# Layer 0 of a two-layer attention kernel: maxima taken by width, narrow units as one event, mask products with a 64-column identity

## The chip, the cores and the metric

One Trainium2 chip, one of its cores. The metric is device microseconds (us) of one execution of the whole program; lower is better. A core has five engines that run their own instruction lists and wait for each other by semaphores: PE (TensorE, matmuls into the PSUM banks), DVE (VectorE), ACT (ScalarE), POOL (GpSimd) and SP (SyncE, which here only issues DMAs).

## The reference, cut to what matters

```python
# B = 2 sequences of T = 1024 tokens, model width 128
x = x + retention(x)                 # 8 heads, not touched by the change
# layer 0: 16 heads of 8 dimensions, causal
scores = jnp.einsum('bhqd,bhkd->bhqk', q, k) / np.sqrt(HEAD_DIM)
scores = jnp.where(causal, scores, -jnp.inf)
attn = jax.nn.softmax(scores, axis=-1)
out = jnp.einsum('bhqk,bhkd->bhqd', attn, v) ...
# then 4 experts (argmax routing)
# layer 1: 16 heads of 8, not causal; two corner scores are set to -1e9
scores = scores.at[:, :, 0, -1].set(NEG)
scores = scores.at[:, :, -1, 0].set(NEG)
weights = jax.nn.softmax(scores, axis=-1)
# then a 128x128 ternary product
```

The layer-0 causal mask matters here: a tile of 128 queries needs only the keys up to its own, so the score blocks have widths of 128, 256, 384 or 512 columns.

## The kernel before, in words

The attention of both layers works in **stacks**: a layer, a batch and a group of four heads. A stack has two **blocks** m, one for each half of 512 queries (`c = m % 2`), so layer 0 has blocks 0 to 15. A block is cut in **units** by tiles of 128 keys: 4 units where c is 0, 8 where c is 1 (layer 1 always has 8). The units of all blocks stand in one list `us`; layer 0 has 96 of them (8 stacks of 12), layer 1 has 128. The loop of `order()` runs over **steps**, one per unit, and writes the program order that PE, ACT and DVE all follow.

In a step s there are, for each of two head pairs x:

- `("S", (s, x))`: PE makes the scores of the unit, keys by queries, two matmuls that stand in the two halves of the array's rows (`par` 0 and 1, one head each; L1525). On the diagonal four more matmuls add the causal mask (L1533): each multiplies 64 rows of two stored tables and adds up to 128 columns. ACT then makes exp of them (L1711), one instruction per head. Three PSUM banks hold scores, so a pair waits for the first exp of the pair before it.
- `("A", (u, x))`: PE makes scores again, queries by keys, for a unit u that lies 12 units ahead (L1453, mask L1460), and DVE reduces them to the maxima (L1886, one instruction for two heads). These go through a **ring** of two slots of two banks each, shared with all other small PE products: a matmul waits until the use two places before it has been read.
- `("V", (s - 1, x))`: PE multiplies the exps of the unit before by V, for one half of the 512 queries (L1559, four heads).

Twelve units are one stack, so unit u of step s is the same unit of the next stack. What `("A", u)` computes is chosen by `maxima_of`: before, blocks with c = 0 take their query tiles upwards (widths 128, 256, 384, 512) and blocks with c = 1 take the two key halves in turn (512, 128, 512, 256, 512, 384, 512, 512). The score units have the widths 512, 384, 256, 128 and five times 512, then 384, 256, 128.

When the maxima of a block are complete, `("M", m)` turns them on PE (L1502), ACT copies them (L1779), POOL splits them in three parts and sends them by three DMAs into the query rows of the stack (L1321). The first score unit of the block waits for these. `("O", m)` (L1567) turns the block's output; the copy of the finished output bank by ACT (L1724) must be done before the first V of the next block. SP loads the query and key rows of later stacks when score counts are reached.

Of the kernel before, what the change touches and what calls it, by code (L numbers as in the profile page):

```python
# [17 lines left out]
P = 128  # L18
# [41 lines left out]
def constants():  # L60
# [131 lines left out]
def build(nc, d, out, phases=5):  # L192
    ctx = ExitStack()
    with ctx:
# [866 lines left out]
        def order():  # L1061
# [75 lines left out]
        def attention():  # L1137
# [263 lines left out]
            def _(pe):  # L1401
# [9 lines left out]
                for kind, k in order():  # L1411
# [21 lines left out]
                    elif kind == "A":  # L1433
# [17 lines left out]
                        for par in range(2):  # L1451
                            rows = slice(HALF * par, HALF * par + SROWS)
                            ins = nc.tensor.matmul(bank(first + par)[:, 0:hi - lo], Qs[k_][rows, qc, x, qo:qo + P],  # L1453
                                                   Ks[k_][rows, x, lo:hi], start=True, stop=not (diag or corner))
                        o = qt * P - lo if diag else (384 if qt == 0 else 0)
                        terms = ((0, 2), (1, 3)) if diag else (((4, 5),) if qt == 0 else ((6, 7),)) if corner else ()
                        for z, (one, two) in enumerate(terms):
                            for par in range(2):
                                rows = slice(HALF * par, HALF * (par + 1))
                                ins = nc.tensor.matmul(bank(first + par)[:, o:o + P], masks[rows, one, :],  # L1460
                                                       masks[rows, two, :], start=False, stop=z == len(terms) - 1)
# [41 lines left out]
                    elif kind == "S":  # L1503
# [9 lines left out]
                        q = HG * s + 2 * x  # L1513
                        ready(pe, exp_done, q + 2 - SCORES)
                        if x == 0 and kt == 0:
                            if m == 1:
                                warm(bank(S_BANK + q % SCORES), 8)
# [5 lines left out]
                        for par in range(2):  # L1523
                            rows = slice(HALF * par, HALF * par + bottom)
# [580 lines left out]
```

## Time and profile before

| | |
|---|---|
| median of 3 runs | 1038.59 us (1037.97 to 1040.91) |
| the profiled execution: time, span | 1032.61 us, 1030.6 us |
| PE busy, share of the span | 905.3 us, 88% |
| DVE | 764.5 us, 74% |
| ACT | 661.7 us, 64% |
| POOL | 391.0 us, 38% |
| mean granted PE clock | 0.965 of 2.4 GHz |
| layer 0's score units | from 294.15 to 627.02 us |

The profile is of one execution; its times are microseconds from the span's start. A busy share says how long an engine had work, not whether the work set the pace. Matmuls overlap, so what counts for PE is the time from one group's start to the next one's start.

### The profile page before, as it was taken

Reading aid. Unit: us, or ns where it says so; the run is one execution under the profiler, and the core shown is the slowest. Engines: PE = TensorE matmul, PEld = TensorE weight load, DVE = VectorE, ACT = ScalarE, POOL = GpSimd, SP = SyncE. Lnnn points to the kernel's source line nnn. Section 1 sums busy time; section 2 is a strip of 40 time slices with the busy share of each in tenths; the row PEclk is TensorE's granted clock in tenths of the full one; section 3 lists DMA queues with packets and bytes.
Section 4 is the critical chain, followed back from the end, with each engine's and each line's share of the span. In section 5 each row is a group of like instructions: output and inputs, shape, how many; then the busy total and the mean of one; then the engine's idle time right before and its main releaser. Section 6 shows DMA issues by size and latency. Waiting matters only on the chain.

```text
span 1030.6 us, 22869 instructions
## 1 busy us (share of the span) xinstructions
PE 905.3 (88%) x9065; PEld 451.3 (44%) x9070; DVE 764.5 (74%) x1187; ACT 661.7 (64%) x1349; POOL 391.0 (38%) x607
## 2 busy tenths in 40 slices
PE   5999999998878888988798878889989999999983
PEld 3778777777523343344373322325422222222232
DVE  3667766856586678867457688796789999999854
ACT  2554565655435677766545647776668988898971
POOL 2755757877332451223444302342423111211240
PEclk8999999999988999999898999999999999999996
DMA  8000000200501034111320431022205100000000
GB/s 291 1 1 2 1 1 2 73 1 2 148 1 41 21 127 136 38 39 37 111 81 23 144 74 37 5 76 91 84 1 169 49 20 20 20 20 2 4 23 21
DMA packets 49405, 52.51 MB, mean 51 GB/s; under 512 B 8874, under 2 KB 40618, under 8 KB 49140
## 3 DMA queue, kind: packets, MB, share of 16 engines
q1 hardware_dynamic: 45012, 48.12, 15.2%
q0 software_dynamic: 4288, 2.94, 1.1%
q8 instruction: 72, 1.18, 0.5%
q14 instruction: 33, 0.27, 0.1%
HBM read 32.37 MB, written 19.68 MB: 51 GB/s over the span
## 4 chain that ended last, share of the span: by engine, by line
PE 50%; DVE 28%; ACT 8%; issue 6%; POOL 3%; DMA 3%; SPq 1%; DVEq 0%; ACTq 0%; POOLq 0%
DVE arena L1886 21%; PE banks L1559 10%; PE banks L1525 7%; PE banks L1453 4%; ACT arena L1711 4%; PE banks L740 3%; PE banks L485 3%; PE banks L495 2%; PE banks L1634 2%; PE banks L1642 2%; PE banks L673 2%; PE banks L735 1%; PE banks L699 1%; ACT arena L521 1%; PE banks L723 1%
## 5 line engine op out<-in xcount | busy, mean ns | idle before, releaser
L1711 ACT ACTIVATE arena<-banks 128x512 f32<-128x512 f32 (+3 forms) x896 | 444.5, 550 | 144.1 <-PE banks L1525 83.9
L1886 DVE TENSOR_REDUCE arena<-banks 128x2 f32<-128x1024 f32 (+1 forms) x448 | 474.8, 1105 | 83.5 <-PE banks L1460 51.5
L1559 PE MATMUL banks<-arena 128*9 128x256 f32 (+1 forms) x3328 | 257.7, 383 | 8.1 <-ACT arena L1724 5.7
L1525 PE MATMUL banks<-arena 61*128 61x512 bf16 (+4 forms) x896 | 170.0, 371 | 29.7 <-ACT arena L1711 26.3
L1453 PE MATMUL banks<-arena 56*128 56x512 bf16 (+3 forms) x896 | 166.7, 366 | 26.8 <-DVE arena L1886 23.3
L1525 PEld LDWEIGHTS banks<-arena 61*128 61x128 bf16 (+1 forms) x896 | 44.8, 93 | 195.0 <-ACT arena L1711 174.5
L1311 POOL CAST arena<-arena 16x128 bf16<-16x128 f32 x32 | 8.9, 279 | 309.3 <-ACT arena L1779 305.3
L1559 PEld LDWEIGHTS banks<-arena 128*9 128x9 f32 x3328 | 50.4, 89 | 134.7 <-issue 83.1
L1453 PEld LDWEIGHTS banks<-arena 56*128 56x128 bf16 x896 | 45.2, 96 | 53.9 <-DVE arena L1886 47.0
L383 POOL TENSOR_TENSOR arena<-arena 128x8 f32<-128x8 f32 (+1 forms) x35 | 51.3, 1466 | 30.8 <-DVE arena L2050 28.4
L1321 POOL DMA_DIRECT2D arena<-arena x96 | 55.1, 577 | 10.7 <-POOL arena L1314 9.2
L521 ACT ACTIVATE arena<-banks,arena 128x128 f32<-128x128 f32 x128 | 46.3, 476 | 0.5 <-PE banks L504 0.5
L1460 PE MATMUL banks<-arena 64*128 64x128 bf16 x576 | 45.4, 226 | 0.0
L511 ACT ACTIVATE arena<-banks 128x1024 f32<-128x1024 f32 x16 | 16.3, 1022 | 39.9 <-PE banks L740 39.9
L1351 POOL DMA_INDIRECT expert_rows<-arena x22 | 21.3, 970 | 54.4 <-DVE arena L1982 54.4
L554 DVE TENSOR_TENSOR arena<-banks,arena 128x128 f32<-128x128 f32 x16 | 4.6, 290 | 47.0 <-PE banks L495 47.0
L1533 PE MATMUL banks<-arena 64*128 64x128 bf16 x512 | 38.8, 219 | 0.0
L529 ACT ACTIVATE arena<-banks 128x1024 f32<-128x1024 f32 x16 | 16.4, 1025 | 33.9 <-PE banks L485 32.6
L767 DVE TENSOR_TENSOR arena<-banks,arena 128x1024 f32<-128x1024 f32 x16 | 19.5, 1221 | 24.2 <-PE banks L673 24.1
L485 PE MATMUL banks<-arena 128*128 128x128 f32 x256 | 34.2, 289 | 2.6 <-DVE arena L770 2.6
L673 PE MATMUL banks<-arena 128*128 128x512 f32 x64 | 33.0, 641 | 1.9 <-DMA arena<-c_gk 1.9
L1460 PEld LDWEIGHTS banks<-arena 64*128 64x128 bf16 x576 | 29.3, 100 | 12.3 <-issue 2.2
(235 smaller groups left out, 1392.6 us busy)
## 6 DMA issues: line engine op xcount, KB each, us to landing
arena<-k_products SPq DMA_DIRECT2D x32, 224.0 KB
arena<-q_products SPq DMA_DIRECT2D x64, 112.0 KB
q_products<-arena SPq DMA_DIRECT2D x16, 384.0 KB, 3.3
k_products<-arena SPq DMA_DIRECT2D x16, 384.0 KB, 3.8
arena<-e_w SPq DMA_DIRECT2D x22, 256.0 KB, 3.1
arena<-arena POOLq DMA_DIRECT2D x96, 4.0 KB, 1.7
sorted_rows<-c_pads SPq DMA_DIRECT2D x2, 709.5 KB, 8.2
arena<-sorted_rows SPq DMA_DIRECT2D x4, 258.0 KB, 3.2
```

The source lines that it names most:

```text
L383: link(eng.tensor_tensor(y, v, epst[:, 1:2].to_broadcast(list(v.shape)), ALU.pow))
L485: ins = nc.tensor.matmul(bank(s // 4)[:, (s % 4) * P:(s % 4 + 1) * P], wg[:, s * P:(s + 1) * P], XT[:, i, :], start=True, stop=True)
L521: ins = nc.scalar.activation(ga[:, s, :], bank(4 + s // 4)[:, (s % 4) * P:(s % 4 + 1) * P], ACT.Identity, scale=gn[:, 0, s:s + 1], bias=gn ...
L673: ins = nc.tensor.matmul(bank(c), XT[:, n + 1, :], wqk[:, c * 512:(c + 1) * 512], start=True, stop=True)
L1321: g_.dma_start(rows, nmp[k % 2][:, i, :]).then_inc(mrow[k % 2], 16)
L1453: ins = nc.tensor.matmul(bank(first + par)[:, 0:hi - lo], Qs[k_][rows, qc, x, qo:qo + P], Ks[k_][rows, x, lo:hi], start=True, stop=not (di ...
L1460: ins = nc.tensor.matmul(bank(first + par)[:, o:o + P], masks[rows, one, :], masks[rows, two, :], start=False, stop=z == len(terms) - 1)
L1525: ins = nc.tensor.matmul(bank(S_BANK + (q + par) % SCORES)[:, o:C], Ks[n % NS][rows, x, kt * P:(kt + 1) * P], Qs[n % NS][rows, c, x, o:C], ...
L1533: ins = nc.tensor.matmul(bank(S_BANK + (q + par) % SCORES)[:, o:o + P], masks[rows, 2 + z, :], masks[rows, z, :], start=False, stop=z == 1)
L1559: ins = nc.tensor.matmul(PS[h * VROWS:h * VROWS + VW, AV_BANK, o:end], V[:, b, kt, HG * g + h, :], Pr[u % PROBS][:, h, o:end], start=(kt = ...
L1711: s_.activation(Pr[s % PROBS][:, h, o:C], bank(S_BANK + q % SCORES)[:, o:C], ACT.Exp) \
L1886: v_.tensor_reduce(of, two_banks, AX.X, ALU.max).then_inc(ring_dve, 1)
```

## The change

Four edits, all in the attention part.

1. `maxima_of` gives layer 0's maxima in the widths 512, 384, 256, 128 (c = 0) and four times 512, then 512, 384, 256, 128 (c = 1). In layer 0 a unit's maxima now have the width of the score unit in the same step, nearly throughout.
2. Units at most 256 wide (`narrow_scan`) put both head pairs into one ring use, one behind the other in each bank: one reduction with four results per partition in place of two. Layer 0 has 32 such units.
3. Score units at most 256 wide (`narrow`) do the same: one pair of banks holds four heads, and ACT makes two exps of 2x256 or 2x128 in place of four. `score_use` numbers the pairs of banks, `exps_of` the counts to wait for.
4. The causal mask is now a table times a 64-column identity: the same number of matmuls, each 64 columns wide in place of 128. The corner masks of layer 1 keep their tables and widths.

```diff
@@ constants()
-        step = HALF * k + lane[:, None] + 1
-        m[:, k] = r[None, :] < step
-        m[:, 2 + k] = np.where(r[None, :] >= step, MASKED, 0)
+        step = HALF * k + lane[:, None]
+        m[:, k] = np.where(step > r[None, :], MASKED, 0)
+        m[:, 2 + k] = np.where(r[None, :] > step, MASKED, 0)
@@ maxima_of
-            return (j, 0) if tiles(m) == QT else (QT * c + j // 2, j % 2)
+            if m < BLOCKS:
+                return (QT * (c + 1) - 1 - j % QT, c if j // QT == c else 0)
+            return QT * c + j // 2, j % 2
@@ new, beside it
+        def narrow(m, kt):
+            lo, hi = queries(m, kt)
+            return hi - lo <= C // 2
+        def narrow_scan(m, j):
+            qt, kc = maxima_of(m, j)
+            return m < BLOCKS and kc == m % 2 and qt % QT < QT // 2
+        score_use, exps_of = {}, []
+        for s, (m, kt) in enumerate(us):
+            for x in range(HG // 2):
+                if x == 0 or not narrow(m, kt):
+                    score_use[s, x] = len(exps_of)
+                    each = 2 if narrow(m, kt) else 1
+                    exps_of += [HG * s + 2 * x + each, HG * s + 2 * x + 2 * each]
@@ order()
-                pairs = [("A", (u, x)) for u in scans.get(s, []) for x in range(2)]
+                pairs = [("A", (u, x)) for u in scans.get(s, []) for x in range(1 if narrow_scan(*us[u]) else 2)]
-                    if 0 <= s < NU:
+                    if (s, x) in score_use:
                         seq.append(("S", (s, x)))
-                    seq += pairs[x * len(pairs) // 2:(x + 1) * len(pairs) // 2]
+                    seq += pairs[(x * len(pairs) + 1) // 2:((x + 1) * len(pairs) + 1) // 2]
@@ PE, "A" and (alike) "S"
+                        for y in range(2) if narrow_scan(m, j) else (x,):
+                            at = y * C // 2 if narrow_scan(m, j) else 0
...
+                            for z in range(2 * diag):
+                                for par in range(2):
+                                    rows, cut = slice(HALF * par, HALF * (par + 1)), at + o + HALF * z
+                                    ins = nc.tensor.matmul(bank(first + par)[:, cut:cut + HALF], masks[rows, z, :],
+                                                           identb[rows, rows], start=False, stop=z == 1)
@@ ACT, "S"
+                            if narrow(m, kt):
+                                s_.activation(Pr[s % PROBS][:, par:HG:2, o:C],
+                                              scores.rearrange("p (y e) -> p y e", y=2)[:, :, 0:C - o], ACT.Exp) \
+                                  .then_inc(exp_done, HG // 2)
@@ DVE, "A"
+                        if both:
+                            v_.tensor_reduce(of, two_banks.rearrange("p r (y e) -> p r y e", y=2)[:, :, :, 0:width],
+                                             AX.X, ALU.max).then_inc(ring_dve, 1)
```

PE's list at the end of block 5, of before: units 6 and 7 (scores 256 and 128 wide, L1525) and the first half of unit 0 of block 6. The maxima (L1453) of these steps are 512 wide, then 128.

```order
L1525 MATMUL banks<-arena 128x256 x2
L1533 MATMUL banks<-arena 128x128 x4
L1453 MATMUL banks<-arena 128x512 x2
L1559 MATMUL banks<-arena 9x256 x4
L1525 MATMUL banks<-arena 128x128 x2
L1533 MATMUL banks<-arena 128x128 x4
L1453 MATMUL banks<-arena 128x512 x2
L1460 MATMUL banks<-arena 128x128 x4
L1525 MATMUL banks<-arena 128x128 x2
L1533 MATMUL banks<-arena 128x128 x4
L1453 MATMUL banks<-arena 128x512 x2
L1460 MATMUL banks<-arena 128x128 x4
```

The same place of the changed kernel, from unit 7 on (L1557 and L1566 are the scores and their mask, L1477 and L1487 the maxima and theirs, L1592 the V products).

```order
L1557 MATMUL banks<-arena 128x128 x2
L1566 MATMUL banks<-arena 128x64 x4
L1557 MATMUL banks<-arena 128x128 x2
L1566 MATMUL banks<-arena 128x64 x4
L1477 MATMUL banks<-arena 128x128 x2
L1487 MATMUL banks<-arena 128x64 x4
L1477 MATMUL banks<-arena 128x128 x2
L1487 MATMUL banks<-arena 128x64 x4
L1592 MATMUL banks<-arena 9x256 x4
L1557 MATMUL banks<-arena 128x512 x2
```

Both head pairs of a narrow unit now stand together, the maxima of the step have shrunk from 512 to 128 columns, and the V products follow without scores between them.

DVE's list around the first steps of the attention, of before: the reductions (L1886), the work for the last retention tile among them (L542 to L1878), and the joining of a block's maxima (L1893).

```order
L1886 TENSOR_REDUCE arena<-banks 128x2 x4
L542 TENSOR_TENSOR arena<-arena 128x1024
L1886 TENSOR_REDUCE arena<-banks 128x2 x2
L554 TENSOR_TENSOR arena<-banks,arena 128x128
L556 BN_STATS arena<-arena 128x6
L557 BN_AGGR arena<-arena 128x2
L1878 MEMSET banks 128x512
L1886 TENSOR_REDUCE arena<-banks 128x2 x2
L1893 TENSOR_TENSOR arena<-arena 128x16
L1886 TENSOR_REDUCE arena<-banks 128x2 x16
```

And of the changed kernel (L1930 is a reduction of one head pair, L1927 one of both).

```order
L1930 TENSOR_REDUCE arena<-banks 128x2 x4
L542 TENSOR_TENSOR arena<-arena 128x1024
L1927 TENSOR_REDUCE arena<-banks 128x4
L554 TENSOR_TENSOR arena<-banks,arena 128x128
L556 BN_STATS arena<-arena 128x6
L557 BN_AGGR arena<-arena 128x2
L1917 MEMSET banks 128x512
L1927 TENSOR_REDUCE arena<-banks 128x4
L1937 TENSOR_TENSOR arena<-arena 128x16
L1930 TENSOR_REDUCE arena<-banks 128x2 x12
```

The four reductions ahead of L542 were 128, 128, 256 and 256 wide and are now 512, 512, 384 and 384; the narrow ones come behind it.

## Rows read from the trace of the kernel before

**Rows 1.** The page: the chain that ended last, by engine.
```profile
PE 50%; DVE 28%; ACT 8%; issue 6%; POOL 3%; DMA 3%; SPq 1%; DVEq 0%; ACTq 0%; POOLq 0%
```

**Rows 2.** By stretch: us, busy PE, PEld, DVE, ACT, POOL; PE clock, DMA.
```profile
396.00:406.00 10.00, 10.00 (x147) 3.95 (x145) 8.59 (x11) 8.13 (x18) 0.02 (x1) 1.00 0.66 208
296.00:306.00 10.00, 8.51 (x91) 3.47 (x93) 8.65 (x11) 5.13 (x12) 1.51 (x5) 0.66 0.01 2
```

**Rows 3.** Timeline, units 2 and 3 of block 5: start, us, engine, line.
```profile
394.59 0.39 PE L1525 MATMUL banks<-arena 59*128 59x512 bf16 x2
396.81 0.39 PE L1525 MATMUL banks<-arena 59*128 59x512 bf16 x2
```

**Rows 4.** Timeline of PE, units 6 and 7 of block 5.
```profile
404.51 0.28 PE L1525 MATMUL banks<-arena 59*128 59x256 bf16 x2
404.63 0.28 PE L1533 MATMUL banks<-arena 64*128 64x128 bf16 x4
404.74 0.38 PE L1453 MATMUL banks<-arena 56*128 56x512 bf16 x2
405.05 0.41 PE L1559 MATMUL banks<-arena 128*9 128x128 f32 x8
405.44 0.28 PE L1525 MATMUL banks<-arena 59*128 59x256 bf16 x2
...
406.54 0.23 PE L1525 MATMUL banks<-arena 59*128 59x128 bf16 x2
...
407.39 0.23 PE L1525 MATMUL banks<-arena 59*128 59x128 bf16 x2 [0.18 <-ACT arena L1711]
...
408.02 0.62 PE L1559 MATMUL banks<-arena 128*9 128x256 f32 x8
```

**Rows 5.** Timeline of PE, unit 0 of block 6 and what follows.
```profile
408.57 0.39 PE L1525 MATMUL banks<-arena 59*128 59x512 bf16 x2
...
409.91 0.39 PE L1525 MATMUL banks<-arena 59*128 59x512 bf16 x2 [0.66 <-ACT arena L1711]
...
411.08 0.34 PE L1525 MATMUL banks<-arena 59*128 59x384 bf16 x2
```

**Rows 6.** Timeline, block 4: M for block 5, its DMAs, units 2, 3, next block.
```profile
381.35 0.28 PE L1502 MATMUL banks<-arena 128*16 128x128 f32 x1
...
384.36 0.28 PE L1525 MATMUL banks<-arena 59*128 59x256 bf16 x2
...
384.56 1.70 POOL L1321 DMA_DIRECT2D arena<-arena  x3 [0.29 <-POOL arena L1314]
...
386.46 0.23 PE L1525 MATMUL banks<-arena 59*128 59x128 bf16 x2
...
389.06 0.39 PE L1525 MATMUL banks<-arena 59*128 59x512 bf16 x2
```

**Rows 7.** Timeline of PE, units 0 and 1 of block 5.
```profile
391.56 0.28 PE L1502 MATMUL banks<-arena 128*16 128x128 f32 x1 [0.33 <-DVE arena L1886]
...
392.69 0.23 PE L1453 MATMUL banks<-arena 56*128 56x128 bf16 x2 [0.53 <-DVE arena L1886]
```

**Rows 8.** Groups by form, 290 to 600 us: count | busy, mean ns.
```profile
L1886 DVE TENSOR_REDUCE arena<-banks 128x2 f32<-128x1024 f32 x95 | 112.3, 1220 | 21.8 <-PE banks L1453 17.2 <-PE banks L1460 3.7
L1886 DVE TENSOR_REDUCE arena<-banks 128x2 f32<-128x256 f32 x29 | 12.3, 424 | 13.2 <-PE banks L1460 13.1
```

**Rows 9.** Timeline: eight matmuls at most 32 columns wide, each with own weights.
```profile
485.85 0.34 PE L1610 MATMUL banks<-arena 128*128 128x32 bf16 x8
```

**Rows 10.** Timeline of PE: waits for DMAs in blocks 11 and 15.
```profile
502.43 0.63 PE L1619 MATMUL banks<-arena 128*128 128x128 f32 x4 [1.53 <-DMA arena<-sorted_rows]
...
596.84 0.61 PE L1453 MATMUL banks<-arena 56*128 56x512 bf16 x4 [0.15 <-DMA arena<-q_products]
```

**Rows 11.** Timeline of PE: M for block 1, and block 1's first unit.
```profile
305.70 0.28 PE L1502 MATMUL banks<-arena 128*16 128x128 f32 x1
...
313.65 0.39 PE L1525 MATMUL banks<-arena 59*128 59x512 bf16 x2 [0.98 <-DMA arena<-arena]
```

More of the change, by code:

```diff
@@ L1450, in _ @@
                         qc, qo = qt // QT, qt % QT * P
[L1451 to L1454, printed above, removed]
                         o = qt * P - lo if diag else (384 if qt == 0 else 0)
-                        terms = ((0, 2), (1, 3)) if diag else (((4, 5),) if qt == 0 else ((6, 7),)) if corner else ()
@@ L1522, in _ @@
                         bottom = MROWS if m < BLOCKS else EROWS
-                        for par in range(2):
-                            rows = slice(HALF * par, HALF * par + bottom)
-                            ins = nc.tensor.matmul(bank(S_BANK + (q + par) % SCORES)[:, o:C],
-                                                   Ks[n % NS][rows, x, kt * P:(kt + 1) * P],
-                                                   Qs[n % NS][rows, c, x, o:C], start=True, stop=not diag)
-                            if not diag:
-                                ins.then_inc(score_done, 1)
@@ L1530, in _ @@
-                        for z in range(2 * diag):
-                            for par in range(2):
-                                rows = slice(HALF * par, HALF * (par + 1))
-                                ins = nc.tensor.matmul(bank(S_BANK + (q + par) % SCORES)[:, o:o + P], masks[rows, 2 + z, :],
-                                                       masks[rows, z, :], start=False, stop=z == 1)
-                                if z == 1:
-                                    ins.then_inc(score_done, 1)
+                        both = narrow(m, kt)
@@ new lines, in _ @@
+                        for y in range(2) if both else (x,):
+                            at = y * C // 2 if both else o
+                            done = HG // 2 if both else 1
+                            for par in range(2):
+                                rows = slice(HALF * par, HALF * par + bottom)
+                                ins = nc.tensor.matmul(bank(S_BANK + (use + par) % SCORES)[:, at:at + C - o],
+                                                       Ks[n % NS][rows, y, kt * P:(kt + 1) * P],
+                                                       Qs[n % NS][rows, c, y, o:C], start=True, stop=not diag)
+                                if not diag:
+                                    ins.then_inc(score_done, 1)
+                            for z in range(2 * diag):
+                                for par in range(2):
+                                    rows = slice(HALF * par, HALF * (par + 1))
+                                    cut = at + HALF * z
+                                    ins = nc.tensor.matmul(bank(S_BANK + (use + par) % SCORES)[:, cut:cut + HALF],
+                                                           masks[rows, 2 + z, :], identb[rows, rows], start=False, stop=z == 1)
+                                    if z == 1 and (y == 1 or not both):
+                                        ins.then_inc(score_done, done)
```

42 lines of the change are left out of this document (26 added, 16 removed).

## The prediction

> **What bounds the kernel now.** I read the page first. The chain that ended last lies half on PE, 28% on DVE and 8% on ACT [rows 1]: no engine sets the pace everywhere, so a busy share can't price this change. I then split layer 0 into stretches. From 396 to 406 us PE is busy throughout, DVE for 8.59 and ACT for 8.13 of 10 us, at the full clock, 2.4 GHz [rows 2]. The reader should see three engines almost equally loaded: an engine that gets a wide piece while another has a narrow one makes the other wait. The timeline shows it step by step. A wide step without masks takes 2.22 us (394.59 to 396.81) [rows 3]; its two reductions take 2.44 us of DVE [rows 8], so DVE only keeps up by catching up elsewhere. The narrow score units 6 and 7 of block 5 take 2.03 us each (404.51 to 406.54 to 408.57) [rows 4, 5], nearly as much as a wide one, though their scores are a half and a quarter as wide. They carry maxima of 512 columns, and in unit 7 PE waits for ACT [rows 4]. In block 4, units 2 and 3 take 2.10 and 2.60 us (384.36, 386.46, 389.06) [rows 6]. Right behind them PE waits for DVE, 0.33 us for M and 0.53 us for a slot of the ring [rows 7]: DVE is still working through wide reductions that it got in the narrow steps.
>
> **PE's prices**, from group start to group start [rows 4]: a 256-wide pair 0.12 us (404.51 to 404.63), a mask group of four 0.11 (to 404.74), a 512-wide pair and the step to V 0.31 (to 405.05). V over 128 queries takes 0.39 (to 405.44), over 256 queries 0.55 (408.02 to 408.57) [rows 4, 5]. By columns a 128-wide pair costs 0.06; each 128 columns are 0.05; the step to V then costs 0.09.
>
> **The mask groups.** They keep four matmuls and four weight loads, and halve the columns. No row shows 64-column groups. If columns set the price, 0.11 becomes 0.055; if the number of instructions does, it stays 0.11. The nearest row has eight matmuls with own weights, at most 32 columns wide, in 0.34 us including the last one's way through the array, some 0.17 by a comparison with the 0.23 of a 128-wide pair [rows 4, 9]; so about 0.02 each, 0.08 for four. I take 0.08, a saving of 0.03 for each group, with 0 and 0.055 as ends.
>
> The trace has the mask group at 0.11 us. The Trainium skill, page "TensorE: Matmul & The Clock Gate", section Back-to-back issue gap, puts a floor of about 25 ns under the distance of two matmuls however few columns they have. By it four masks would cost 0.10 us, and the halved columns would give almost nothing; no run shown so far has the 64-column form.
>
> **The steps of a stack, one by one.**
> - Unit 6 of an odd block: scores 2x0.12, maxima 2x0.12 (they were 512 wide), four mask groups at 0.08, 0.09, V 0.39+0.55: 1.83 against 2.03, saves 0.20.
> - Unit 7: 2x0.06, 2x0.06, 4x0.08, 0.09, 0.55: 1.20 against 2.03, saves 0.83. The next scores wait for the first exp of this unit; from scores through exp to scores took 1.34 us at 512 columns (408.57 to 409.91 [rows 5]), and this exp has 256 elements, so the chain should end before 1.20.
> - Units 2 and 3 of an even block are the same two: 1.83 against 2.10 and 1.20 plus 0.57 (O, by 2.60 less 2.03) against 2.60: save 0.27 and 0.83.
> - Unit 0 of an even block: 2.51 us (408.57 to 411.08), its first half bound by scores, exp, scores (the 0.66 us wait for ACT [rows 5]). Maxima grow from 128 to 512 columns: +0.16 in the half that is not covered, masks -0.09: +0.07. Unit 1: 256 becomes 384 and masks shrink: 0.
> - Units 0 and 1 of an odd block: DVE has now had a 256- and a 128-wide unit before, so both waits for it (0.86 us together [rows 7]) can go; but V of unit 1 then waits for ACT's copy of the finished output, which starts behind the same exps. I take 0.45, between 0 and 0.86.
> - Units 2 and 3: the masked 256-wide maxima become unmasked 512 ones, +0.10 and -0.11: 0. Units 4 and 5: masks, 0.06 and 0.12.
>
> An even block saves 1.03 us, an odd one 1.66, a stack 2.7. Merging by itself removes the fixed part of 32 reductions and 64 exps (two 256-element reductions take 0.85 us [rows 8]); it lies beside PE's work in these steps and is costed at nothing. Were PE no cover, it would be worth some 0.2 us in each narrow unit.
>
> **What lies in the way.** The narrow steps hid the chain of M. M for block 5 stands at 381.35, its DMAs at 384.56, the block's scores at 389.06: 7.71 us [rows 6]. Mine leaves 7.71-0.27-0.83 = 6.6. The chain itself takes 3.21 us to the DMAs and 1.70 to issue them, 4.9, and then the landing, for which at most 2.8 us were left; so it needs between 4.9 and 7.7 us. I take the middle, 6.3: just covered. At the upper end an odd block would lose 1.1 us.
>
> **The sum over layer 0.** Stacks 1 to 4 save 2.7 each: 10.8. In stack 5, PE waits 1.53 us for the sorted rows [rows 10]; POOL's scatter sets that, so what units 2 and 3 of block 10 and unit 0 of block 11 save before it (1.4) only lengthens the wait: 1.3 is left. In stack 6, what comes after block 13's unit 6 is lost: layer 1's first maxima wait for a store and a load (0.15 us at 596.84 [rows 10]), and faster steps meet that wait: 1.9 is left. Stack 7 gives nothing: it runs under that chain, and then under layer 1's double scans, which DVE bounds. In stack 0, block 1 saves 1.7. Block 0 saves nothing: its steps end in a wait for M's DMAs, 7.95 us behind M (305.70 to 313.65) [rows 11]. DVE gets 2048 elements more before the last retention tile's work (widths 128 and 256 become 512 and 384), at (1220-424)/768 = 1.04 ns each [rows 8] 2.1 us, and as many fewer behind it. I take 0 for that, with 2 us either way.
>
> Total: 10.8+1.3+1.9+1.7 = 15.7 us. Against the profiled execution's 1032.6 us that is 1016.9; the median of the runs is 6.0 us above it, so 1022.9, say 1023.
>
> **Rivals.**
> - *Half of it* (20%): 3 to 10 us, 1028 to 1035. Masks that stay at 0.11 take 0.03 from some 28 groups in each of six stacks, 5 us; DVE, which then bounds units 0 to 5 of odd blocks (2.44 us a unit against 2.22), keeps the 0.45, 3 us more; M's chain could come on top. For it: three engines this evenly loaded leave a gain on one little room. Against it: unit 7's 0.83 rests on columns that are simply gone from there.
> - *Nothing* (5%): the program keeps its columns but for the masks, so if PE's columns were the whole price, moving them would give only 0.03 a group, and the ring's order could eat that. Against it: unit 7 and unit 3 hold waits and maxima that don't come back elsewhere in full, since a step bound by ACT or DVE takes the wider maxima in its slack [rows 5, 7].
> - *Slower* (4%): PE's clock. Between 296 and 306 us the mean grant is 0.66, a mixture of 1.2 and 2.4 GHz, after PE had waited for ACT and DVE; ten such microseconds hold 3.4 us of lost clock [rows 2]. If narrower matmuls made the clock fall in blocks that now run at 2.4 GHz, one such stretch in a block would cost up to 3.4 us. From five of them in fourteen blocks on, the change loses. Against it: the steps get shorter by losing waits, and 396 to 406 us runs at 1.00 with these waits near it.
>
> The Trainium skill's page "TensorE: Matmul & The Clock Gate", section Part 1, says that the throttled clock is the default and activity releases it. By that rule fuller narrow steps should keep the clock; the 0.66 stretch agrees as far as it goes.
> - *More* (8%): over 23 us saved, 1015 or less. The mask groups go to 0.055 (4 us more), both DVE waits go whole (3 us), and the start gains 2.
>
> **How the numbers follow.** The forecast's own case, 10 to 23 us saved, has 63%. The unknown mask price alone moves the sum by 5 us down or 4 up, the start by 2, the DVE waits by 3. The range leaves out under 1 in 10 on each side: 1013 to 1032. A change of 0.3% (3.1 us) is about what a measurement of this kernel can tell. Faster by more than that: 63+8 and 20 of the half case, 91%; same 5%; slower 4%.
>
> **What the changed profile would show.** Reductions: 416 in place of 448, 16 of them 1024 and 16 of them 512 elements in four results. Unit 6 of a steady odd block near 1.8 us and unit 7 near 1.2; unit 3 of an even one near 1.8; the waits for DVE in units 0 and 1 gone or moved to ACT's copy. Mask groups 0.08 us from start to start. The wait for sorted rows longer, near 3 us. Layer 1 unchanged in length from its first maxima on. I am wrong if units 1 to 3 of odd blocks grow past 2.4 us (DVE is then the bound), if block starts wait for M's DMAs by 0.5 us or more, or if the clock column falls below 1.00 in blocks 3 to 9.

## The result and the profile after

| | before | after |
|---|---|---|
| median (lowest to highest) | 1038.28 us (1036.71 to 1040.91, 4 runs) | 1023.83 us (1023.12 to 1026.3, 4 runs) |
| ratio | | 0.9857, 95% interval 0.9829 to 0.9885 |
| profiled execution, its span | 1032.61, 1030.6 us | 1024.54, 1022.1 us |
| mean granted PE clock of it | 0.965 | 0.957 |

The change saves 14.5 us between the medians. The profiled executions differ by only 8.1 us: the one of before is 5.7 us below its median, and the one of after holds a stall of 4.7 us in layer 1 that other executions of the same kernel don't have (below). Measured again beside the kernel before, the change saved 16.0 us and, another time, 10.8 us, so the size of the gain is itself uncertain by some microseconds. The page of after, its chain by engine and its groups:

```profile
PE 50%; DVE 27%; ACT 7%; issue 6%; DMA 4%; POOL 3%; SPq 2%; another core or an unknown queue 1%; DVEq 0%; ACTq 0%; POOLq 0%
...
L1930 DVE TENSOR_REDUCE arena<-banks 128x2 f32<-128x1024 f32 (+1 forms) x384 | 440.9, 1198 | 65.4 <-PE banks L1477 33.0
...
L1927 DVE TENSOR_REDUCE arena<-banks 128x4 f32<-128x1024 f32 (+1 forms) x32 | 30.4, 954 | 16.2 <-PE banks L1487 13.5
L1746 ACT ACTIVATE arena<-banks 128x512 f32<-128x512 f32 (+1 forms) x64 | 27.9, 490 | 17.2 <-PE banks L1566 16.9
```

384 and 32 are the 416 reductions that were expected; the chain keeps its shares [rows 1]. Units 6 and 7 of block 5 and the start of block 6, timeline of PE (answers to [rows 4, 5]):

```profile
398.23 0.28 PE L1557 MATMUL banks<-arena 59*128 59x256 bf16 x2
398.35 0.22 PE L1566 MATMUL banks<-arena 64*128 64x64 bf16 x4
398.41 0.27 PE L1557 MATMUL banks<-arena 59*128 59x256 bf16 x2
...
399.02 0.84 PE L1592 MATMUL banks<-arena 128*9 128x128 f32 x16
399.79 0.23 PE L1557 MATMUL banks<-arena 59*128 59x128 bf16 x2
399.86 0.22 PE L1566 MATMUL banks<-arena 64*128 64x64 bf16 x4
399.92 0.22 PE L1557 MATMUL banks<-arena 59*128 59x128 bf16 x2
...
400.37 0.62 PE L1592 MATMUL banks<-arena 128*9 128x256 f32 x8
400.92 0.39 PE L1557 MATMUL banks<-arena 59*128 59x512 bf16 x2
```

Unit 6 now takes 1.56 us and unit 7 1.13, without a wait. From a mask group to what follows it are 0.06 us (398.35 to 398.41, 399.86 to 399.92). Blocks 4 and 5, timeline of all engines (answers to [rows 6, 7]):

```profile
376.97 0.28 PE L1529 MATMUL banks<-arena 128*16 128x128 f32 x1
...
379.99 1.71 POOL L1341 DMA_DIRECT2D arena<-arena  x3 [0.29 <-POOL arena L1334]
380.08 0.28 PE L1557 MATMUL banks<-arena 59*128 59x256 bf16 x2
...
380.98 2.04 DVE L1927 TENSOR_REDUCE arena<-banks 128x4 f32<-128x1024 f32 x2 [0.38 <-PE banks L1487]
...
381.64 0.23 PE L1557 MATMUL banks<-arena 59*128 59x128 bf16 x2
...
383.36 0.39 PE L1557 MATMUL banks<-arena 59*128 59x512 bf16 x2
...
384.58 0.39 PE L1557 MATMUL banks<-arena 59*128 59x512 bf16 x2 [0.62 <-ACT arena L1750]
...
385.46 0.28 PE L1529 MATMUL banks<-arena 128*16 128x128 f32 x1
...
386.51 0.39 PE L1477 MATMUL banks<-arena 56*128 56x512 bf16 x2 [0.45 <-DVE arena L1930]
```

Units 2 and 3 of block 4 take 1.56 and 1.72 us. DVE has nothing to do ahead of their maxima (0.38 us idle) and is done with them at 383.02, before block 5 begins. The M that stands in block 5 (block 6's, at 385.46) no longer waits; the ring still costs 0.45 us a unit later. M's chain for block 5 now has 6.39 us (376.97 to 383.36), and this block's scores don't wait for its DMAs. By stretch, ten microseconds of the wide units 30 to 34, before and after (us, busy PE, PEld, DVE, ACT, POOL, clock, DMA):

```profile
394.10:404.10 10.00, 10.00 (x136) 3.64 (x137) 8.01 (x11) 8.61 (x17) 1.68 (x3) 1.00 0.70 219
388.00:398.00 10.00, 10.00 (x140) 3.40 (x140) 9.72 (x12) 8.71 (x18) 2.03 (x4) 1.00 0.75 224
```

DVE is at 9.72 of 10 us where it was at 8.01 in the same units: the wide units are now DVE's as much as PE's. Further on in layer 0, timeline of PE (answers to [rows 10]):

```profile
438.78 0.39 PE L1557 MATMUL banks<-arena 59*128 59x512 bf16 x2 [0.71 <-DMA arena<-arena]
...
464.69 2.65 PE L1631 MATMUL banks<-arena 128*128 128x4 f32 x16 [0.77 <-DVE arena L1930]
...
490.29 1.96 PE L1652 MATMUL banks<-arena 128*128 128x128 f32 x8 [0.79 <-DMA arena<-sorted_rows]
...
539.63 0.39 PE L1557 MATMUL banks<-arena 59*128 59x512 bf16 x2 [1.21 <-DMA arena<-arena]
...
578.24 0.39 PE L1557 MATMUL banks<-arena 59*128 59x512 bf16 x2 [1.32 <-DMA arena<-arena]
...
583.33 1.04 PE L1477 MATMUL banks<-arena 56*128 56x512 bf16 x4 [2.42 <-DMA arena<-q_products]
```

The lines at 438.78, 539.63 and 578.24 are the first scores of blocks 9, 13 and 15. They wait 0.71, 1.21 and 1.32 us for M's DMAs, where in the trace of before only block 1 has such a wait, 0.98 us [rows 11]. The wait for the sorted rows is 0.79 us here, where 3 were expected; layer 1's first maxima wait 2.42 us (0.15 before), as was expected. In unit 60 the gating product (L1631) waits for a wide reduction, and in this execution the stretch then runs at 1.2 GHz for longer than before (stack 5 below). And in layer 1, timeline of all engines, and two stretches:

```profile
671.41 0.96 POOL L1358 DMA_INDIRECT sorted_rows<-arena  x1 [0.30 <-issue]
672.68 0.96 POOL L1358 DMA_INDIRECT sorted_rows<-arena  x1 [0.30 <-issue]
673.58 1.09 ACT L1750 ACTIVATE arena<-banks 128x512 f32<-128x512 f32 x2 [3.51 <-remote]
673.66 1.23 DVE L1930 TENSOR_REDUCE arena<-banks 128x2 f32<-128x1024 f32 x1 [1.16 <-issue]
...
674.23 0.61 PE L1557 MATMUL banks<-arena 61*128 61x512 bf16 x2 [3.29 <-issue]
```

```profile
670.00:680.00 10.00, 5.82 (x44) 1.07 (x40) 6.01 (x10) 3.34 (x8) 5.85 (x5) 0.70 0.35 102
675.00:680.00 5.00, 4.11 (x30) 0.67 (x26) 2.45 (x2) 2.18 (x5) 1.94 (x1) 0.50 0.54 151
```

PE stands for 3.29 us, ACT for 3.51 and DVE for 1.16 at its end; the trace names no instruction that releases them ("issue", "remote"). Then PE has 1.2 GHz for some 7 us (0.52 from 674 to 681). Units 113 and 114 take 11.5 us instead of 6.8. The profile of before has no such place.

### The profile page after: what moved, and what is told of

It is laid out like the page before. It is cut to its first block, busy times and chain, and to the rows that moved or that the text cites. A ratio compares the mean times of both kernels' runs of the same rounds, so it can differ in the third digit from the quotient of the medians.

```text
span 1022.1 us, 22793 instructions
## 1 busy us (share of the span) xinstructions
PE 890.6 (87%) x9065; PEld 445.1 (44%) x9070; DVE 762.3 (75%) x1155; ACT 655.0 (64%) x1285; POOL 392.0 (38%) x607
## 4 chain that ended last, share of the span: by engine, by line
PE 50%; DVE 27%; ACT 7%; issue 6%; DMA 4%; POOL 3%; SPq 2%; another core or an unknown queue 1%; DVEq 0%; ACTq 0%; POOLq 0%
DVE arena L1930 19%; PE banks L1592 10%; PE banks L1557 7%; PE banks L1477 5%; ACT arena L1750 3%; PE banks L740 3%; PE banks L485 3%; PE banks L495 2%; PE banks L1667 2%; PE banks L1675 2%; PE banks L673 2%; DMA arena<-arena 1%; PE banks L735 1%; PE banks L699 1%; ACT arena L521 1%
## 5 line engine op out<-in xcount | busy, mean ns | idle before, releaser
L1930 DVE TENSOR_REDUCE arena<-banks 128x2 f32<-128x1024 f32 (+1 forms) x384 | 440.9, 1198 | 65.4 <-PE banks L1477 33.0
L1750 ACT ACTIVATE arena<-banks 128x512 f32<-128x512 f32 (+1 forms) x768 | 409.4, 587 | 120.9 <-PE banks L1557 77.7
L1592 PE MATMUL banks<-arena 128*9 128x256 f32 (+1 forms) x3328 | 257.0, 385 | 6.8 <-ACT arena L1763 4.6
L1557 PE MATMUL banks<-arena 61*128 61x512 bf16 (+4 forms) x896 | 167.5, 373 | 33.9 <-ACT arena L1750 23.7
L1477 PE MATMUL banks<-arena 56*128 56x512 bf16 (+3 forms) x896 | 165.2, 371 | 29.1 <-DVE arena L1930 22.1
L1557 PEld LDWEIGHTS banks<-arena 61*128 61x128 bf16 (+1 forms) x896 | 44.7, 93 | 194.5 <-ACT arena L1750 160.8
L1592 PEld LDWEIGHTS banks<-arena 128*9 128x9 f32 x3328 | 51.6, 89 | 133.0 <-issue 86.7
L1477 PEld LDWEIGHTS banks<-arena 56*128 56x128 bf16 x896 | 45.2, 95 | 54.6 <-DVE arena L1930 40.9
L1927 DVE TENSOR_REDUCE arena<-banks 128x4 f32<-128x1024 f32 (+1 forms) x32 | 30.4, 954 | 16.2 <-PE banks L1487 13.5
L1746 ACT ACTIVATE arena<-banks 128x512 f32<-128x512 f32 (+1 forms) x64 | 27.9, 490 | 17.2 <-PE banks L1566 16.9
L767 DVE TENSOR_TENSOR arena<-banks,arena 128x1024 f32<-128x1024 f32 x16 | 19.6, 1223 | 24.0 <-PE banks L673 23.9
L866 POOL TENSOR_TENSOR arena<-arena 128x512 f32<-128x512 f32 x16 | 25.3, 1578 | 22.5 <-DVE arena L770 22.5
```

The lines of the kernel that those rows point to most:

```text
L1477: ins = nc.tensor.matmul(bank(first + par)[:, at:at + hi - lo], Qs[k_][rows, qc, y, qo:qo + P], Ks[k_][rows, y, lo:hi], start=True, stop=n ...
L1557: ins = nc.tensor.matmul(bank(S_BANK + (use + par) % SCORES)[:, at:at + C - o], Ks[n % NS][rows, y, kt * P:(kt + 1) * P], Qs[n % NS][rows, ...
L1592: ins = nc.tensor.matmul(PS[h * VROWS:h * VROWS + VW, AV_BANK, o:end], V[:, b, kt, HG * g + h, :], Pr[u % PROBS][:, h, o:end], start=(kt = ...
L1750: s_.activation(Pr[s % PROBS][:, 2 * x + par, o:C], scores[:, o:C], ACT.Exp) \
L1927: v_.tensor_reduce(of, two_banks.rearrange("p r (y e) -> p r y e", y=2)[:, :, :, 0:width], AX.X, ALU.max).then_inc(ring_dve, 1)
L1930: v_.tensor_reduce(of[:, :, x], two_banks[:, :, 0:width], AX.X, ALU.max).then_inc(ring_dve, 1)
```

## The experiments

Units count the score units from 0; layer 0 is 0 to 95, a stack twelve of them. Their lengths are read in each trace's timeline from one unit's first scores to the next one's, so a wait ahead of a unit's first scores stands in the length of the unit before it. 24 to 59 are the three steadiest stacks. Even one program's traces differ outside them: units 0 to 11 took 42.4 to 43.4 us in four traces of kernels that are alike there and 45.1 in a fifth, and units 12 to 23 of the changed kernel 37.4, 38.7 and 36.3.

Eight kernels separate the three parts of the change: order of widths, merging (scores and maxima), masks. What the parts undo:

```diff
@@ order of widths undone
-            if m < BLOCKS:
-                return (QT * (c + 1) - 1 - j % QT, c if j // QT == c else 0)
-            return QT * c + j // 2, j % 2
+            return (j, 0) if tiles(m) == QT else (QT * c + j // 2, j % 2)
@@ merging undone: narrow, narrow_scan
-            return hi - lo <= C // 2
+            return False
...
-            return m < BLOCKS and kc == m % 2 and qt % QT < QT // 2
+            return False
@@ masks undone: the tables of before, 128 columns
-                                                           identb[rows, rows], start=False, stop=z == 1)
+                                                           masks[rows, 2 + z, :], start=False, stop=z == 1)
```

### Each part alone, and the changed kernel again

**Order of widths alone.** 

> The kernel before with the new order of widths alone (maxima of layer 0 in the order 512, 384, 256, 128), no merged units, old masks. Theory A (a narrow step must be narrow on every engine; each edit gives its own part): a steady stack of 12 units, 29.5 us before, gets 1.2 us shorter by the waits for DVE and the smaller maxima in units 6 and 7, 6 us in all: ratio 0.994. Theory B (the masks did the work): within 1 us of before, 1.000. Theory C (merging did it): also 1.000.

**Masks alone.** 

> The kernel before with the 64-column mask products alone. The trace after shows a mask group of four at about 0.06 us in place of 0.11. Theory A: 32 groups a stack of which some 20 stand on PE's path, 0.05 us each, 1 us a stack, 6 us in all: ratio 0.994. Theory B: most of the gain, 10 us or more, 0.990. Theory C: under 3 us, 0.998.

**Merging alone.** 

> The kernel before with merged narrow units alone (scores and maxima), old order of widths and old masks. Theory A: merging without aligned widths leaves the wide maxima in the narrow steps, so unit 7 falls only from 2.03 to about 1.8 us: 2 us in all, ratio 0.998. Theory C (merging did it, by fewer instructions and fewer rounds of scores, exp, scores): 8 us or more, 0.992.

**All three, again.** 

> The changed kernel once more, unchanged. Its first trace shows a stretch of 3.3 us at 670.9 us in which PE, ACT and DVE all stand without a wait for one another, followed by some 5 us at 1.2 GHz; 4.9 us were lost there against the trace of before at the same units. Theory: this is an accident of that one execution and not of the change. Then this trace has no such stretch at unit 113 and its layer 1 is within 1 us of that of before (some 8 us to the end saved become 12 to 13). Rival: the change causes it; then it stands at the same unit again. Ratio 0.986 either way.

| kernel | median us | ratio (95%) | units 24 to 59 | unit 34 | unit 35 |
|---|---|---|---|---|---|
| before | 1040.0 | | 96.37 | 2.03 | 2.03 |
| widths alone | 1038.7 | 1.000 (0.9979 to 1.002) | 94.11 | 2.03 | 1.86 |
| masks alone | 1034.69 | 0.9946 (0.9929 to 0.9964) | 95.00 | 1.92 | 2.03 |
| merging alone | 1036.56 | 0.9975 (0.996 to 0.999) | 96.73 | 1.98 | 2.40 |
| all | 1024.03 | 0.9846 (0.9821 to 0.9871) | 86.46 | 1.56 | 1.13 |

By the medians' differences the three save 1.3+5.3+3.4 = 10.0 us, and all together 16.0. In the steady stacks it is plainer: 2.3 and 1.4 saved and 0.4 lost make 3.3, against 9.9 (with masks alone, unit 41 holds a chance stall of 1.1 us; without it the parts make 4.4). Widths alone missed the 0.994 that was expected: they gave 0.75 us a steady stack and not 1.2, and nothing in the time. Merging alone has the time that was expected, but it makes unit 7 of an odd block longer (2.40 us) where 1.8 was expected. DVE and PE there, kernel with merging alone, timelines of the two engines:

```profile
401.00 4.62 DVE L1927 TENSOR_REDUCE arena<-banks 128x2 f32<-128x1024 f32 x4 [0.36 <-PE banks L1475]
```

```profile
402.10 0.23 PE L1555 MATMUL banks<-arena 59*128 59x128 bf16 x2
402.17 0.28 PE L1563 MATMUL banks<-arena 64*128 64x128 bf16 x4
402.28 0.22 PE L1555 MATMUL banks<-arena 59*128 59x128 bf16 x2
402.34 0.28 PE L1563 MATMUL banks<-arena 64*128 64x128 bf16 x4
402.45 0.38 PE L1475 MATMUL banks<-arena 56*128 56x512 bf16 x2
...
403.51 0.39 PE L1475 MATMUL banks<-arena 56*128 56x512 bf16 x2 [0.56 <-ACT arena L1743]
...
404.50 0.39 PE L1555 MATMUL banks<-arena 59*128 59x512 bf16 x2
```

PE is done with the merged scores in 0.35 us and then stands at the second 512-wide maxima. The trace names ACT as the releaser, but DVE is the one without a gap: four wide reductions from 401.00 to 405.62. So I read the wait as one for DVE's wide maxima: what merging takes off PE and ACT, they don't let through. With the widths alone the opposite engine holds unit 35, timeline of PE:

```profile
409.81 0.23 PE L1557 MATMUL banks<-arena 59*128 59x128 bf16 x2
...
410.67 0.23 PE L1557 MATMUL banks<-arena 59*128 59x128 bf16 x2 [0.34 <-ACT arena L1749]
...
411.67 0.39 PE L1557 MATMUL banks<-arena 59*128 59x512 bf16 x2
```

The second pair waits for ACT's exps (four short ones). Each edit alone opens one of two gates that stand in the same unit.

The repetition of the changed kernel was expected to have no stall at unit 113, as an accident of one execution. It has it, in the same place and as long (3.27 us of PE), and so have the profiles of the three kernels with one part. By this group of runs alone the stall could be the program's; the third profile of the changed kernel, below, has none.

### All but one part

**Masks as before.** 

> The changed kernel with the old 128-column mask products. Theory A (the edits add up): loses the masks' 6 us of 14.5, ratio to before 0.992. Theory B (masks did it): within 3 us of before, 0.997 or more. If the columns of the masks were covered in the new order: still 0.986.

**Widths as before.** 

> The changed kernel with the old order of widths (merged narrow units and 64-column masks stay). Theory A: the narrow score steps carry 512-wide maxima again and DVE's waits come back: 7 us of 14.5 left, ratio 0.993. If the order of widths is of no account: 0.986.

**No merging.** 

> The changed kernel without merged units (new order, new masks). Theory A: in unit 7 the second head pair's scores must wait for the first one's exp (some 0.8 us from scores through exp to scores), so the unit takes about 1.6 us in place of 1.13, unit 6 about 1.75 in place of 1.56; four such units a stack, 1.3 us a stack, 7 us in all: ratio 0.993. If merging only saves instructions that lie beside other work: 0.986 to 0.988.

**Scores merged, maxima not.** 

> The changed kernel with merged scores but maxima in two uses of the ring also where narrow. If what merging gives is the score-exp-score round: 0.986 to 0.988, near the changed kernel. If it is the ring and DVE's fixed cost: near the run without any merging.

| kernel | median us | ratio (95%) | units 24 to 59 | unit 34 | unit 35 |
|---|---|---|---|---|---|
| before | 1033.72 | | 96.37 | 2.03 | 2.03 |
| all but masks | 1026.48 | 0.9911 (0.9886 to 0.9937) | 89.90 | 1.77 | 1.35 |
| all but widths | 1022.8 | 0.9898 (0.9871 to 0.9925) | 94.52 | 1.87 | 2.34 |
| all but merging | 1027.04 | 0.9932 (0.9911 to 0.9953) | 90.64 | 1.87 | 1.70 |
| all but merged maxima | 1023.98 | 0.99 (0.9879 to 0.992) | 87.30 | 1.78 | 1.17 |

(Rows of before in units are those of its one profile. The profile of all but widths holds a chance stall of 1 us in unit 29.) The changed kernel itself wasn't timed beside these four, so only their steady stacks are set against its own. Measured against the 86.5 us of all parts, the last part added is worth 3.4 us (masks), 4.2 (merging) and 8.0 (widths; 7 without the stall) in three steady stacks. Merging of the maxima is worth 0.8 of the 4.2, so the merged scores carry most of it: merging costed at nothing was wrong. In the time, undoing the masks or the merging cost what was expected (0.992 and 0.993). The widths' 7 to 8 us are not seen in the time: all but widths is as fast as any of these four, 0.9898, where 0.993 was expected. Part of them the new order gives back outside the steady stacks: units 60 to 95 sum to 149.0 us without it and to 153.2, 153.5 and 151.2 us in the three profiles of the changed kernel, 2.2 to 4.5 us more. Where the rest goes isn't shown: the profiled execution of all but widths (1022.63 us) is 6.2 us above the third one of the changed kernel, which has no stall either.

### The old order where steps are crowded

In the first trace with the new order, units 7, 12, 19, 60 and 66 are longer than before (3.12 to 4.47, 3.69 to 4.54, 3.60 to 4.56, 4.61 to 6.19, 7.27 to 8.71 us). All stand in steps that also hold retention, gating or gather work, and in all but unit 66 the maxima have grown from 128 or 256 to 512 columns; those of unit 66 had 512 before, and units 65 and 67 beside it got them. Three kernels timed side by side:

```diff
@@ maxima_of
+            if m < BLOCKS and (m >= 12):        # the other kernel: m in (3, 13, 15)
+                return (j, 0) if tiles(m) == QT else (QT * c + j // 2, j % 2)
             if m < BLOCKS:
```

**Old order in blocks 12 to 15.** 

> The changed kernel, but the maxima of blocks 12 to 15 (which stand in units 60 to 83, beside the wide gathers and the loading of layer 1's queries) keep the old order of widths; masks and merging as after. Theory A (a wide reduction of maxima put into a step that is already crowded lengthens it, so the new order gives back there what it gains in the steady stacks): units 60 to 83 shorten by 2 to 4 us (unit 60 from 6.2 to about 4.1, unit 66 from 8.7 to about 7.0, unit 79 from 5.3 to 4.7), unit 63 lengthens again (2.0 to 3.9), and the time is 1.5 to 4 us below the changed kernel's. Theory B (stacks 5 to 7 are held by the scatters and loads of GpSimd's queue, and what one unit saves another waits): units 60 to 95 sum to the same within 1 us, and so does the time. Theory C (the aligned order is worth its steady 3 us in every stack): the time is 3 to 5 us above the changed kernel's.

**Old order in blocks 3, 13 and 15.** 

> The changed kernel, but the maxima of blocks 3, 13 and 15 alone (units 4 to 11, 64 to 71, 76 to 83) keep the old order of widths. These are the blocks for which the sums of the units were shorter without the new order (23.2 against 25.0, 55.8 against 57.8, 27.5 against 28.2 us). Theory A (crowded steps): those sums are had again, 4.5 us together, and the time is 3 to 4.5 us below the changed kernel's, lower than with the late blocks alone. Theory B (queue-bound late stacks): only the early 1.8 us is had, less if the later start of the gathers waits anyway: 0 to 2 us. Theory C: 2 to 4 us above the changed kernel's.

**The changed kernel a third time.** 

> The changed kernel once more, as the measure for the other two on the same chip: 0.985 to 0.990 of the kernel before by every theory. Its profile shows whether the stall near unit 113 comes and goes without a change of the program (theory: it does, and costs 4 to 5 us where it comes).

| kernel | median us (lowest to highest) | ratio to before, 1032.08 (95%) | units 60 to 83 | 84 to 95 |
|---|---|---|---|---|
| changed kernel | 1021.29 (1016.46 to 1022.07) | 0.9882 (0.9862 to 0.9902) | 105.3 | 45.8 |
| old order, 12 to 15 | 1014.96 (1014.62 to 1017.51) | 0.9831 (0.9813 to 0.9848) | 104.3 | 44.0 |
| old order, 3, 13, 15 | 1020.93 (1019.91 to 1021.92) | 0.988 (0.9863 to 0.9898) | 108.3 | 44.7 |

The late blocks' old order is faster than the changed kernel, with intervals that don't meet. The 6.3 us between the medians are more than the 1.5 to 4 us expected by theory A, and the traces show only 2.9 us of it in units 60 to 95. The two profiled executions don't show the gain as a whole (1016.46 and 1017.5 us): the one with the old order took 3.2 us more in units 0 to 23, where the kernels are alike. Timeline of PE there, unit 60:

```profile
463.62 0.39 PE L1559 MATMUL banks<-arena 59*128 59x512 bf16 x2
...
466.02 1.85 PE L1633 MATMUL banks<-arena 128*128 128x4 f32 x16
...
467.80 0.34 PE L1559 MATMUL banks<-arena 59*128 59x384 bf16 x2
```

The gating product starts 2.40 us into the unit, without a wait for DVE, and takes 1.85 us; in the changed kernel it starts 3.61 us in (461.08 to 464.69; 460.00 to 463.61 in the third profile, behind the same 0.77 us wait for DVE) and takes 2.65 (2.04 in the third). POOL's first scatter waits for the places that DVE works out from the gating's results (L1987 and L1989), and PE for the rows that it sorts, in the changed kernel's third profile and then in this one, timelines of POOL and PE:

```profile
473.34 1.09 POOL L1358 DMA_INDIRECT sorted_rows<-arena  x1 [5.89 <-DVE arena L1987]
487.51 2.22 PE L1652 MATMUL banks<-arena 128*128 128x128 f32 x8 [5.36 <-DMA arena<-sorted_rows]
```

```profile
475.06 1.09 POOL L1360 DMA_INDIRECT sorted_rows<-arena  x1 [3.95 <-DVE arena L1989]
489.48 1.99 PE L1654 MATMUL banks<-arena 128*128 128x128 f32 x8 [3.60 <-DMA arena<-sorted_rows]
```

The scatter starts 13.34 us behind the start of unit 60 in the changed kernel (14.87 and 13.39 in its other two profiles) and 11.44 with the old order (12.98 in the kernel before), and units 60 to 67 together take 43.6 and 41.0 us. A second place is block 15: with the old order in the late blocks its first scores no longer wait for M's DMAs (2.42 us in the third profile), and units 84 to 87, which have the same pieces in both kernels, take 9.12 us in place of 10.40. Block 13's wait is gone too, but units 72 to 75 are no shorter for it (10.55 and 10.63 us). The clock by stretch in the changed kernel's first profile, then in this one:

```profile
460.00:480.00 20.00, 16.25 (x201) 9.36 (x201) 12.89 (x37) 10.80 (x23) 6.28 (x11) 0.81 0.16 49
480.00:500.00 20.00, 15.64 (x96) 5.16 (x97) 9.06 (x16) 8.14 (x16) 10.18 (x14) 0.59 0.39 111
```

```profile
460.00:480.00 20.00, 16.05 (x244) 8.68 (x235) 14.37 (x39) 10.77 (x24) 9.47 (x14) 0.90 0.22 58
480.00:500.00 20.00, 14.56 (x133) 7.53 (x131) 8.06 (x18) 10.46 (x22) 9.25 (x13) 0.85 0.40 119
```

The changed kernel ran mostly at 1.2 GHz between 480 and 500 us (0.59); but its third profile had 0.83 there, so chance has a part in it.

Of blocks 3, 13 and 15 theory A fell. Its expectation also rests on sums that I had added wrongly: the units' lengths give 24.1 against 25.0, 51.8 against 53.8 and 29.3 against 28.2 us, so 1.8 us was there to be had and not 4.5. Even these didn't come; the time fell by 0.4 us, as theory B had it (0 to 2). Units 6 and 7 went back from 3.47 and 4.47 to 2.78 and 3.05 us, but unit 5 rose from 2.80 to 3.68 and units 10 and 11 from 1.88 and 2.08 to 2.19 and 3.03: units 4 to 11 took 24.97 against 24.98 us. In units 76 to 83, where block 15's maxima stand, the old order cost 2.3 us (31.4 against 29.1), and the 1.5 us that units 64 to 71 had won with blocks 12 to 15 (51.1 against 52.6) stayed away (53.0). One unit's length is no measure of an order; the sum over the block is.

**The late blocks' version once more.** 

> The kernel with the old order of widths in blocks 12 to 15 once more, in another call. Its five executions lay at 1014.6 to 1017.5 us with granted clocks of 0.965 to 0.970; those of the changed kernel beside them at 1016.5 and 1017.8 us with 0.965 and above, and at 1021.3 to 1022.1 with 0.955 to 0.962. Theory A (the late blocks' order is worth 6 us, in the program): ratio to the kernel before 0.981 to 0.985 again, and no execution at a clock of 0.962 or less. Theory B (the order is worth some 2 us, and the other 4 us are the stall of some executions, which that call happened not to show for it): executions at both clocks, some 5 us apart, and a ratio of 0.984 to 0.987. The profile shows units 60 to 71 at 64 to 65 us (changed kernel 65.6 to 68.3) by both.

It took 1016.13 us (1014.61 to 1018.48, 6 runs) beside 1033.73 of before: 0.984, 0.981 to 0.9871. Units 60 to 71 took 64.4 us. None of its 11 executions had a mean clock of 0.962 or less; of the changed kernel's 15, 13 had. The ratio alone would fit both theories; executions at a low clock, which B expected, didn't come, so the clocks speak for A. Beside the changed kernel this version was timed once, and won; against the kernel before it won twice. Of its 6 us, 2.9 are steps that are seen to be shorter. The rest isn't explained. A low mean clock is no sign of the stall at unit 113: the kernel with blocks 3, 13 and 15 in the old order has 0.958 in its profile without that stall, and merging alone 0.966 with it.

## Why the prediction was right, and where its terms were off

The time, 1023.83 us, lies 0.8 us from the 1023 predicted and is faster than before by far more than 0.3%. Part of that is luck: terms cancel, and in the third group of runs the same change saved 10.8 us between the medians, near the low end of the 10 to 23 us of the main case. The mechanism of the steady stacks, narrow steps that become narrow on every engine, came as told. Step by step, for the steady stack of blocks 4 and 5 (units 24 to 35):

| units | predicted | measured |
|---|---|---|
| even 0, 1 | +0.07, 0 | +0.06, +0.12 |
| even 2, 3 | -0.27, -0.83 | -0.54, -0.88 |
| odd 0 and 1 | -0.45 | -0.42 |
| odd 2, 3 | 0, 0 | 0, -0.02 |
| odd 4, 5 | -0.06, -0.12 | +0.06, -0.21 |
| odd 6, 7 | -0.20, -0.83 | -0.47, -0.90 |
| a stack | -2.7 | -3.2 |

- **Mask groups**: taken at 0.08 us, they are 0.06, near the lower bound (0.055). This is the first mis-sized term. Masks back to 128 columns in the changed kernel lengthen unit 34 by 0.21 us for four groups, 0.05 each: columns set the whole price down to 64.
- **Unit 6 and even unit 2**: V's sixteen matmuls, now in one piece, take 0.77 us (399.02 to 399.79) where I added 0.39 and 0.55. This and the masks make the missing 0.27.
- **Merging at nothing**: wrong as a price. I took unit 7's 1.20 as PE's columns and called merging a bystander; without merging unit 35 stands at 1.70, where, as in the kernel with the widths alone, PE waits for ACT's exps (0.40 us ahead of the second pair). The result of the unit was right, its attribution not.
- **DVE's waits**: M's went, the ring's stayed at 0.45 us, together what was taken. **M's chain**: "just covered" held in the steady blocks and failed in others. In blocks 5 and 7 the last of M's three DMAs landed 5.8 and 5.9 us behind M, with 6.4 and 6.3 us left. For blocks 9, 13 and 15 it landed 7.6, 7.7 and 8.3 us behind M (6.1, 6.8 and 6.6 before), and their first scores waited: 0.71, 1.21 and 1.32 us in the first profile, 0.45, 1.78 and 2.42 in the third. This is the sign of being wrong that was named, block starts that wait 0.5 us or more. It came, and the sum held all the same, since stack 4 gained 3.2 us in spite of it. The failed step is the one value of 6.3 us for every block, taken from block 5. For block 13 the DMAs were also issued later (4.80 us behind M, 3.91 before); why those of blocks 9 and 15 land later is open.
- **Start and stack 1**: stack 0 gained 4.4 us where 1.7 were taken (units 0 to 11 from 46.78 to 42.38), and stack 1 0.7 where 2.7 were (38.13 to 37.44; 1.9 in the third profile). The sign of the 2 us of DVE work at the start was left open, and it fell on the good side: units 1 and 3 end earlier. Part is chance: unit 5 took 4.08 us before and 2.81 after, and 4.29 in a kernel that is the same as after there. Stack 1's failed step is the transfer of the steady stack to steps that also hold retention work: wide maxima lengthen units 12 and 19 (by 0.85 and 0.96 us). Unit 17's 1.45 us more are chance, since the third profile doesn't have them.
- **Stack 5**: -1.3 expected, +1.8 measured (66.51 to 68.32), -0.9 in the third profile. The step that failed: that the scatter's start is fixed, so that faster units only lengthen the wait for the sorted rows. The scatter hangs on the gating work that starts in unit 60. With wide maxima there it starts 13.3 to 14.9 us into the stack (13.0 before), and 11.4 where the late blocks keep the old order. The wait itself was 0.79 us in the first profile, where units 60 to 66 ran longer and much at 1.2 GHz, and 5.36 in the third, around the 3 expected. Stacks 6 and 7 gave nothing (85.08 to 84.91; -0.5 in the third profile), 1.9 were taken: the wait for layer 1's rows grew by 2.27 us as said, and the waits of blocks 13 and 15 for M's DMAs, which had been nothing, came on top.
- **Layer 1**: its length was to stay. In the profile it grew by 4.6 us (374.65 to 379.24 from the start of unit 96 to that of the last, 223), all in the stall at unit 113. The third profile of the same program has no stall, 373.70 us, and its execution took 1016.46 us: 16.1 below the profiled execution of before, where the sum said 15.7.

So between two executions without the stall, picked from many, the sum was right to half a microsecond, by terms that cancel: in that third profile stacks 2 to 4 were under-counted by 2.1 us and the start by 2.0, the crowded stacks 1, 5, 6 and 7 over-counted by 3.6 (6.8 in the first). The slower rival didn't come: in blocks 4 to 9 the clock stays at 1.00. In block 3, which the named sign also took in, PE had 1.2 GHz for 3.4 us in the first profile and for none in the third. The rival's mechanism showed in stack 5: PE had 1.2 GHz for 23.9 us of units 60 to 71 in the first profile and for 20.5 in the second, against 13.7 before; but 10.2 in the third, so it doesn't come in every execution. Of the signs of being wrong, one was badly set: units 1 and 3 of odd blocks were to stay under 2.4 us, but had 2.82 before and have 2.80 and 2.81 now, so they didn't grow.

## What to carry to other kernels

Look for the narrow steps whose score, exp and maxima pieces come from different widths, and line up all engines' widths and event counts together: here each alone gave 1 to 5 us (the 1 within the noise), all three 16. Check the new order against every step that carries foreign work, by sums over a block, and leave the old order where those sums are not shorter; that gave the fastest kernel here. Steps that get shorter also uncover the chains that they hid, so look at the first scores of every block and not of one: M's DMAs left blocks 5 and 7 alone and held up 9, 13 and 15. And one profile can hold a stall worth a third of the gain, so compare several executions of the same kernel before reading a difference.

## What the runs showed of the hardware

- Four mask matmuls of 64 columns, two in each half of the array's rows and each with its own weights, take 0.06 us from group start to the next group's start (398.35 to 398.41, 399.86 to 399.92), 0.015 each. The Trainium skill, "TensorE: Matmul & The Clock Gate", section Back-to-back issue gap, has a floor of about 25 ns between matmuls; the trace doesn't agree if all four count one by one. It would nearly, if the two halves of the rows count apart: two matmuls in each half would then take 0.05 us, an estimate from that page's figure. No run here separates the halves.
- The stall at unit 113 (PE 3.29, ACT 3.51, DVE 1.16 us, then 1.2 GHz) is in the profiles of the changed kernel, of its repetition and of each part alone, and in none of those taken later (all but one part, old orders, third time), nor in that of before. The changed kernel shows it twice and once not, so it isn't fixed by the program. It lengthens units 113 and 114 together from 6.8 to 11.5 us. The kernel before, whose one profile has no stall, had medians of 1038.3 and 1040.0 us beside the kernels that show it and 1032.1 to 1033.7 us beside those that don't; whether it had the stall there too, no profile shows. POOL's scatters go on during it, and the trace names no transfer that an instruction waits for there. Its cause stays open.
- The same three DMAs of M, issued 3.0 to 3.4 us behind M, had landed 5.8 to 5.9 us behind it in blocks 5 and 7 and only 7.6 and 8.3 us behind it in blocks 9 and 15 of the changed kernel's first profile.
